# A graph layer with a gated delta rule: the chunk inverse carries L·T from level to level, key products in one, outputs behind the state

## The reference, cut to what matters

```python
def step(S, x):
    qt, kt, vt, bt, gt = x
    S = S * jnp.exp(gt)[..., None, None]
    kv = jnp.einsum('bhk,ebhkv->ebhv', kt, S)
    delta = (vt[None] - kv) * bt[..., None]
    S = S + kt[None, :, :, :, None] * delta[..., None, :]
    ot = jnp.einsum('bhk,ebhkv->ebhv', qt * scale, S)
    return (S, ot)
```

## Time and profile before

| | |
|---|---|
| three runs | 991.96, 995.42 (median), 997.62 us |
| span of the profiled execution | 993.7 us |
| PE busy | 894.7 us (90%), 12598 matmul records |
| DVE, ACT, POOL busy | 600.3, 254.6, 369.8 us |
| first transposes of the delta loop to its last output matmul | 562.8 to 924.6 us |

### The profile page before, as it was taken

One profiled execution on the slowest core, in us unless ns is written; L12 is line 12 of the kernel. 1 busy time (PEld: TensorE's weight loads), 2 busy tenths in 40 slices (PEclk: granted clock), 3 DMA queues, 4 the chain that ended last, 5 costly groups with the idle time before them and its releaser, 6 DMA issues.

```text
span 993.7 us, 28569 instructions
## 1 busy us (share of the span) xinstructions
PE 894.7 (90%) x12598; PEld 577.6 (58%) x12598; DVE 600.3 (60%) x1288; ACT 254.6 (26%) x502; POOL 369.8 (37%) x303
## 2 busy tenths in 40 slices
PE   3999999999998999999999888888888888888598
PEld 1454453445665444444444478788788788887343
DVE  7799999958884323236075555545555555554274
ACT  1121112201221000032122244333333343333331
POOL 5021100000111200002899576564565646542582
PEclk9999999999999999999999999999999999999989
DMA  8300000120000600000166843433434334321452
GB/s 258 121 1 1 1 1 1 43 63 1 1 2 3 231 1 1 0 1 2 16 244 258 275 124 99 124 105 94 117 99 120 99 101 118 99 57 35 116 145 65
DMA packets 74869, 80.59 MB, mean 81 GB/s; under 512 B 34437, under 2 KB 57655, under 8 KB 74743
## 3 DMA queue, kind: packets, MB, share of 16 engines
q1 hardware_dynamic: 69623, 57.58, 21.1%
q0 software_dynamic: 5120, 21.14, 6.0%
HBM read 54.25 MB, written 24.39 MB: 79 GB/s over the span
## 4 chain that ended last, share of the span: by engine, by line
PE 68%; POOL 11%; DVE 9%; issue 8%; DMA 1%; ACT 1%; SPq 0%; DVEq 0%; POOLq 0%
PE bank L829 16%; PE bank L760 9%; PE bank L530 7%; PE bank L563 4%; PE bank L549 3%; POOL nrm L1274 3%; POOL qkv_slots L1279 2%; PE bank L751 2%; DVE rows L1570 2%; PE bank L930 2%; PE bank L1003 2%; PE bank L919 2%; POOL gb_slots L1269 2%; PE bank L906 2%; PE bank L944 2%
## 5 line engine op out<-in xcount | busy, mean ns | idle before, releaser
L751 PE MATMUL bank<-W,xT 128*128 128x512 f32 x296 | 128.3, 593 | 0.0
L751 PEld LDWEIGHTS bank<-W,xT 128*128 128x128 f32 x296 | 56.0, 190 | 69.9 <-issue 69.7
L829 PE MATMUL bank<-big 64*64 64x64 f32 x2240 | 84.6, 222 | 6.4 <-issue 5.5
L760 PE MATMUL bank<-hs,big 125*125 125x512 f32 x200 | 86.6, 593 | 0.0
L829 PEld LDWEIGHTS bank<-big 64*64 64x64 f32 x2240 | 75.9, 137 | 8.2 <-issue 7.2
L530 PE MATMUL bank<-W,xT 128*125 128x512 f32 x160 | 79.3, 615 | 0.0
L1255 POOL TENSOR_TENSOR big<-big,ident_sb 125x125 f32<-125x125 f32 x10 | 11.4, 1141 | 173.9 <-ACT big L1066 173.9
L829 PE MATMUL bank<-tB 64*64 64x64 f16 x2560 | 59.5, 195 | 16.8 <-issue 12.2
L1314 POOL TENSOR_TENSOR tB<-tA,masks_sb 128x512 f16<-128x512 f16 x20 | 39.3, 1967 | 92.8 <-DVE tA L1816 92.8
L1831 DVE TENSOR_TENSOR tB<-bank,masks_sb 128x512 f16<-128x512 f32 x80 | 54.7, 684 | 21.2 <-PE bank L829 21.1
L760 PEld LDWEIGHTS bank<-hs,big 125*125 125x125 f32 x200 | 37.3, 188 | 47.7 <-issue 47.5
(11 more groups left out here) (302 smaller groups left out, 1874.1 us busy)
## 6 DMA issues: line engine op xcount, KB each, us to landing
big<-qkv_slots SPq DMA_DIRECT2D x40, 256.0 KB, 3.6
rows<-step_rows SPq DMA_DIRECT2D x40, 128.0 KB, 3.5
rows<-gam_rows SPq DMA_DIRECT2D x40, 128.0 KB, 3.3
big<-qkv_slots SPq DMA_DIRECT2D x80, 64.0 KB, 2.7
big<-qkv_slots SPq DMA_DIRECT2D x40, 128.0 KB, 3.0
o_slots<-big SPq DMA_DIRECT2D x40, 128.0 KB, 2.5
x_all<-in_x SPq DMA_DIRECT2D x10, 224.0 KB
out<-tC SPq DMA_DIRECT2D x10, 224.0 KB
```

The costliest lines, as they stand in the source:

```text
L751: last = mm(bank[:, b0, :], xT[:, k, t * P:t * P + 128], W[:, w, k, :], start=(k == 0), stop=(k == KC - 1))
L760: last = mm(bank[0:P, t % 2, :], cnt[:, s, t * P:(t + 1) * P], hs[:, s, :], start=(s == 0), stop=(s == NT - 1))
L829: last = mm(bank[q, b0, a * CL:(a + 1) * CL], lhsT[q, a, :], rhs[q, a, :], start=True, stop=True)
```

## The change

1. **Inverse.** `untranspose` and `level_m` of level 1 are gone. `pairs` is now two DVE operations: `TT16` by a mask, and `B16[0]` by DVE's transposition of 32x32 blocks. `first_m` forms L·T, `first_mt` its transpose; from then on M = L·T is carried: `level_up` forms the next M from M's transpose (`MT16`) and `B`, and in the same step the next `TT16` and `MT16` side by side with one 128-wide product for a matmul. Only the last level forms T itself. ACT's two copies for a level become one of 1024 columns (`keep_tm`), and for level 3 one of 512.
2. **Key products.** `kBD` holds the keys of two heads on the diagonal of a 128x128 matrix (zeroed once by DVE, refilled by two ACT copies on 64 partitions for a unit); 8 matmuls of 128x128x128 against keys and queries side by side replace the 32 of `key_key` and `key_query`.
3. **Outputs.** `outputs` is split into `state_part` and `out_part`; the outputs of a unit's second chunk are made one round later, and SP has a round more.
4. **Orders.** The rounds of all engines are rewritten; POOL no longer makes `TT16`; `T0`, `TT` and `RES` have one buffer in place of two.

```diff
+            def key_products(u):
+                s = u % 2
                 pe.wait_ge(S["kF_done"], u + 1)
+                pe.wait_ge(S["qF_done"], u + 1)
+                for a in range(8):
+                    last = mm(pair_of_banks(s, a), kBD[:, a, :], kqF[s][:, a, :, :].rearrange("p w n -> p (w n)"), start=True, stop=True)
+                last.then_inc(S["kk_psum"], 1)
...
+            def level_up(u, lv):
+                s = u % 2
+                B = B16[lv % 2][s]
+                pe.wait_ge(S["b_done"], level_count(u, lv))
+                pe.wait_ge(S["tm_done"], level_count(u, lv))
+                products(MB[s], MT16[s], B).then_inc(S["m_psum"], 1)
+                if lv == LEVELS - 2:
+                    products(TTB[s], B, TT16[s]).then_inc(S["tm_psum"], 1)
                 else:
-                    pe.wait_ge(S["t_done"], level_count(u, lv - 1))
-                products(MB[s], AT16[s], T16[s]).then_inc(S["m_psum"], 1)
+                    for a in range(8):
+                        for b in range(2):
+                            q = slice(CL * b, CL * b + CL)
+                            last = mm(pair_of_banks(s, a)[q, :], B[q, a, :], TM[s][q, a, :, :].rearrange("p w n -> p (w n)"), start=True, stop=True)
+                    last.then_inc(S["tm_psum"], 1)
...
             for h in range(NSC + 2):
+                unit_of(level_up, h - 1, 3)
+                unit_of(key_products, h)
                 chunk_of(old_keys, h, 0)
+                unit_of(last_level, h - 1)
+                if h >= 3:
+                    out_part(2 * (h - 3) + 1)
                 chunk_of(solve, h, 0)
+                unit_of(residual, h - 1)
+                chunk_of(state_part, h, 0)
+                unit_of(first_m, h)
+                unit_of(features, h + 1)
+                unit_of(first_fix, h - 1)
+                unit_of(first_mt, h)
                 chunk_of(old_keys, h, 1)
+                unit_of(level_up, h, 1)
                 chunk_of(solve, h, 1)
                 unit_of(second_fix, h - 1)
+                chunk_of(out_part, h, 0)
+                chunk_of(state_part, h, 1)
+                unit_of(level_up, h, 2)
+            out_part(NCK - 1)
...
+                for b in range(2):
+                    q = slice(CL * b, CL * b + CL)
+                    A(kBD[q, :, q], bank[q, TB[s], :].rearrange("p (a n) -> p a n", n=CL), ACT.Copy)
...
+            def keep_tm(u, lv):
+                s = u % 2
+                act.wait_ge(S["tm_psum"], level_count(u, lv + 1))
+                if lv == LEVELS - 2:
+                    A(TT16[s], bank[:, TTB[s], :].rearrange("p (a n) -> p a n", n=CL), ACT.Copy).then_inc(S["tm_done"], 1)
+                else:
+                    A(TM[s].rearrange("p (z a) w n -> p z (a w n)", z=2), bank[:, TB[s]:TTB[s] + 1, :], ACT.Copy).then_inc(S["tm_done"], 1)
...
+            def pairs(u):
...
+                V.tensor_tensor(TT16[s], AT16[s], bm(level0T, 8), ALU.mult).then_inc(S["tt1_done"], 1)
+                dve.wait_ge(S["tt1_done"], u + 1)
+                V.transpose(B16[0][s], TT16[s]).then_inc(S["t16_done"], 1)
```

More of the change, by code:

```diff
@@ L257, in gps_layer @@
         vp = [unit(big, 16 + s) for s in range(2)]
-        kF = [unit(big, 22 + s) for s in range(2)]
-        qF = [unit(xTu, s) for s in range(2)]
+        kqF = [buf[:, n * D:(n + 2) * D].rearrange("p (a w n) -> p a w n", w=2, n=CL) for buf, n in ((big, 22), (xTu, 0))]
+        kF, qF = ([f[:, :, w, :] for f in kqF] for w in range(2))
+        kBD = big[:, 5 * D:7 * D].rearrange("p (a n) -> p a n", n=2 * CL)
         kG = [[unit(xTu, 2 + 2 * p + s) for s in range(2)] for p in range(2)]
@@ L471, in _ @@
                 load_kp(0, c)
-            for h in range(NSC + 2):
+            for h in range(NSC + 3):
                 if h + 2 < NSC:
@@ L871, in level_t, with first_mt @@
[L871 to L877, removed]
+                pe.wait_ge(S["t16_done"], u + 1)
+                products(MB[s], AT16[s], B16[0][s]).then_inc(S["m_psum"], 1)
+            def first_mt(u):
+                s = u % 2
+                pe.wait_ge(S["pt_done"], u + 1)
+                products(TB[s], B16[0][s], AT16[s]).then_inc(S["tm_psum"], 1)
@@ L878, in level_t, with last_level @@
+            def last_level(u):
+                s, lv = u % 2, LEVELS - 1
+                B = B16[lv % 2][s]
                 pe.wait_ge(S["b_done"], level_count(u, lv))
-                products(TB[s], TT16[s], B16[s]).then_inc(S["t_psum"], 1)
-                products(TTB[s], B16[s], TT16[s]).then_inc(S["tt_psum"], 1)
+                pe.wait_ge(S["tm_done"], level_count(u, lv))
+                products(TB[s], TT16[s], B).then_inc(S["t_psum"], 1)
+                products(TTB[s], B, TT16[s]).then_inc(S["tt_psum"], 1)
@@ L896, in second_fix @@
                 pe.wait_ge(S["uu_done"], u + 1)
-                products(MB[s], RES[s], UU[s]).then_inc(S["tf_psum"], 1)
+                products(MB[s], RES, UU).then_inc(S["tf_psum"], 1)
             def old_keys(c):
@@ L921, in solve, with state_part @@
                 last.then_inc(S["z_psum"], 1)
-            def outputs(c):
+            def state_part(c):
                 u, c2 = c // 2, c % 2
@@ L1830, in level_b @@
                 dve.wait_ge(S["m_psum"], level_count(u, lv))
-                V.tensor_tensor(B16[s], pm(MB[s]), bm(level[lv], 8), ALU.mult).then_inc(S["b_done"], 1)
+                V.tensor_tensor(B16[lv % 2][s], pm(MB[s]), bm(level[lv], 8), ALU.mult).then_inc(S["b_done"], 1)
             def residual(u):
@@ L1871, in _ @@
                 gate_rows(t)
+            dve.wait_ge(S["first_scattered"], 64)
+            dve.wait_ge(S["rest_scattered"], 32 * (NT - 2))
+            V.memset(kBD, 0.0).then_inc(S["filled"], 1)
             for h in range(NSC + 2):
-                unit_of(level_b, h - 1, 3)
+                unit_of(level_b, h - 1, 4)
                 unit_of(lower, h)
@@ L1876, in _ @@
                 unit_of(lower16, h)
-                unit_of(decay_matrix, h + 1)
-                unit_of(level_b, h - 1, 4)
-                unit_of(pairs, h)
-                chunk_of(new_state, h, 0)
-                chunk_of(right_side, h, 1)
-                unit_of(level_b, h, 1)
-                unit_of(scores, h)
-                unit_of(residual, h - 1)
-                unit_of(first_fix, h - 1)
-                unit_of(level_b, h, 2)
-                chunk_of(new_state, h, 1)
-                unit_of(second_fix, h - 1)
+                unit_of(pairs, h)
+                unit_of(residual, h - 1)
+                chunk_of(new_state, h, 0)
+                unit_of(scores, h)
+                unit_of(level_b, h, 1)
+                unit_of(first_fix, h - 1)
+                chunk_of(right_side, h, 1)
+                unit_of(level_b, h, 2)
+                unit_of(second_fix, h - 1)
+                chunk_of(new_state, h, 1)
+                unit_of(decay_matrix, h + 1)
+                unit_of(level_b, h, 3)
             def mix_rows(t):
```

165 lines of the change are left out of this document (72 added, 93 removed).

## The result

The changed kernel takes **1016.75 us** (median of 4 runs, 1014.31 to 1025.99); the kernel before took 993.69 beside it. The ratio is 1.0257 with a 95% interval of 1.0214 to 1.0299 (the quotient of the two medians alone is 1.023): 2.6% slower, where 1.0% faster was forecast and 1003 was the range's upper end. The profiled execution has a span of 1015.9 us against 993.7.

A forecast was written before the change was run, and what follows sets the result against it. PE was taken as bound by its number of instructions; a unit of 17.0 us instead of 17.8 gave 993.7 - 12.5 + 2 + 0.5 = 983.7 span, so 985.4 us, range 970 to 1003.

The forecast's parts named there:

- code bounds the loop before: Delta loop before: PE bound by arriving instructions, 127 matmul records per 4.2 us, 17.7 us a unit.
- PE's work: PE's own issue time in a unit of the changed loop: 13.7 us, against 13.9 before.
- Key products: PE's 16 new float32 records of 128x128 in a unit: 2.0 us, against 1.92 before.
- wait A: PE before level_up 1, waiting for ACT's copy MT16: 1.1 us a unit.
- wait B: PE before level_up 3, waiting for DVE's level 3 mask and ACT's 1024-wide copy: 1.8 us a unit.
- the edit at nothing: TT16's mask and the block transposition on DVE: 0.68 us each, done 0.7 before first_m, little cost in the steady part.
- wait C: PE before first_m, waiting for DVE's block transposition: not forecast, 0.60 us in the changed kernel's trace.
- 0.4 a unit for pauses: PE's stops for code in the changed loop: about one in a unit, 0.4 us.
- clock rival: Two waits a unit bring the clock to 0.91 all through the loop: unit 18.4, kernel about 1007 us; chance 0.13.
- the 17.0: Forecast length in us of a unit of the changed loop, 0.8 less than before.
- the start, +2: First rounds: kBD copies, qF and DVE's operations lengthen the hand-overs; 2 us more, bounds 0 and +4.
- the end, +0.5: Last round: 0.5 us more for the late state_part; last outputs otherwise at 0.

The follow-up runs named there:

- run with half the columns: Kernel before the change, with the 64x64x64 products of the inverse cut to 32 columns; 1010.32 us, ratio 1.023.
- all three edits: Changed kernel with add_eye released behind DVE's mask, second_fix between level_up 2 and 3, key products one head at a time without kBD; 966.28 us, ratio 0.973.
- first edit: Changed kernel with POOL's add_eye waiting for TT16 instead of AT16; 998.81 us, ratio 1.0069.
- waits filled: Changed kernel with seven unused matmuls in the first round, plus one each in wait A and wait B of each round; 997.52 us, ratio 1.007.
- all three edits and the filled start: Kernel with all three edits, plus seven unused matmuls of 512 float32 columns in the first round alone; 963.0 us, ratio 0.9707.
- run with the filled start: Changed kernel as it is, plus seven unused matmuls of 512 float32 columns in its first round; 1009.08 us, ratio 1.016.

## Why the prediction was wrong

**Right: code bounds the loop before, and the number of records sets it.** The run with half the columns does not show this by its time, since PE's issue time hardly fell in it. What shows it are the stops, 126 or 127 records apart in the earlier trace rows and with half the columns alike, and the kernel with all three edits: 378 records in 12.58 us with a wait among them, and units of 15.1 and 15.2 for 456 records.

**Right: PE's work, waits A and B.** Key products 2.0 against 2.0. Counted by issue as the forecast was: work 13.8 against 13.7, wait A 1.3 against 1.1, wait B 1.7 against 1.8.

**Wrong, and the largest part: the edit at nothing.** "On DVE the mask lasts 0.68 ... Both end 0.7 us before PE comes to `first_m`." It lasts 1.79, since POOL's `add_eye` is released by the same semaphore and reads SBUF at the same time. The upper bound of 2.0 was named, but got no price; 1.1 us more against a slack of 0.7 is already a wait, and the rest of wait C is hand-over. The forecast had 16.6 for a unit without a stop for code (13.7 + 1.1 + 1.8); it is 17.55. Of these 0.95 us, wait C is 0.8, so 16 x 0.8 = 13 us, and the first edit gave back just that (17.55 to 16.76). The Trainium skill (SBUF — State Buffer, Who interferes with whom) says that a DVE instruction with two SBUF inputs and a GpSimd one that reads SBUF block one another, and that the one that starts first keeps the port for its whole length. The trace agrees in each order: DVE ends 0.55 after POOL when POOL is first, and where DVE was first, in the first round (the pair of rows from 569 us), it took 0.69 and POOL 1.77 instead of 1.27. I had not applied that rule.

**Wrong: 0.4 a unit for pauses.** That is 6.4 us for the 16 units; what they take beyond 16 x 17.55 is 292.6 - 280.8 = 11.8. The four units of 18.2 to 18.4, each with one stop for code, hold 2.9 of it: a stop comes in every second unit and not in each, but wait B follows it in full. The three late units of 20.0, 20.2 and 21.4 hold 8.8. The clock rival named such dips, at 0.91 all through; they came as a few deep ones (0.98 over the stretch), no more than before had in its own 16 units, but they did not go away as the 17.0 assumed. The kernel before has 284.1 - 16 x 17.2 = 8.9 beyond its clean unit of the earlier trace rows, so the forecast also let part of the old pauses vanish without a reason.

**Wrong: the start, +2.** It is +9.0. With the waits filled it is 39.3 at clock 1.00, so 4.9 of the 9.0 belong to the clock (0.85 in the changed kernel); 4.1 are left, just above the upper bound of +4, and the kernel before was itself at 0.95. Dropping the block-diagonal part alone gives 39.5, at clock 0.83, so this part with its two copies lies on the path, as forecast. Of those 4.7 us less, its own price is about what the forecast had: at full clock the first two units take 9.1 and 14.4 with it (filled waits), 7.8 and 13.1 without it (all three edits and the filled start; the first unit takes 7.8 without the other two edits as well), 1.2 and 1.3 against the forecast's 1.5 in each.

**Wrong: the end, +0.5.** It is +5.7. The kernel before had clock 1.00 there and the changed one 0.96. With the changed kernel's own waits but at clock 1.00 (the run with the filled start) it is 45.7, so 2.5 of the 5.7 go with the clock. The filled waits can't tell: they end ahead of the last rounds, and the end is 48.3 at 0.96 there too. With waits B and C reduced, at clock 1.00, it is 43.5, so these two are 2.2; about 1 us is open.

By these steps the miss in the loop is 33.2 us (+23.2 instead of -10.0): 7.0 at the start, 5.2 at the end, 21.0 in the units. Of the 21.0, 15.2 are the unit without a stop (16 x 0.95, most of it wait C, then wait A), 5.4 the pauses (11.8 against 6.4), and 0.4 rounding in the forecast. That the kernel might be slower had a chance of 0.14, put down to the clock; the chief cause was the wait that had been set at nothing.

**By part of the change.** The levels' part has fewer records and one hop, as forecast; it was not tried alone. The block-diagonal product saves 16 records a unit, 0.5 us of code by 4.2 us for 127, and costs two copies on ACT, 1.0, ahead of the one PE waits for; without it the kernel is 29.5 us faster. The new place of `second_fix` opened wait B: moved, it gives 21.4. `TT16` on DVE met POOL: parted, it gives 17.9. All three put right give 50.5 and not the sum of 68.8, since what bounds the loop then is code, and the rest of the change is then worth 2.7% against the kernel before.

## What to carry to other kernels

Write down for each term whether it stands in every unit or only in some: here the unit without a stop and the pauses of the others missed by different amounts, for different reasons. Before an operation is moved to VectorE with both inputs in SBUF, look at what the same semaphore releases on GpSimd; a few hundredths of a microsecond decided here which of the two waited for the other, DVE for 1.1 us or POOL for 0.5. Once an engine that was bound by its code gets fewer instructions, each new hand-over has to be covered by other work, or the gain turns into idle time. And before a run with less work is read, look at whether the work became less: half the columns left the pitch of the records as it was.

## What the runs showed of the hardware

- *A kernel gets faster by useless work.* Seven unused matmuls in the first round took the granted clock there from 0.82 to 1.00 and the stretch from 38.3 to 34.6 us; two more in each round took the changed kernel, with those seven in, from 1009.08 to 997.52, and from 1016.75 without any.
- *Fewer columns can be slower.* 32 columns instead of 64 left the pitch of float32 records at 0.028 against 0.030 us, but the clock went from 0.98 to 0.91 over the 16 units and from 0.95 to 0.60 at the start, and the kernel took 18 us more.
- *Code arrives at a rate.* 126 or 127 matmul records, each with its weight load, for 4.2 us, in one kernel with and one without waits among them; a wait of 0.60 in 378 records cost nothing beside that.
- *The order of two starts decides the price.* A DVE operation of 0.69 took 1.79 when POOL's started 0.03 earlier; POOL's took 1.77 instead of 1.27 when DVE's was 0.04 earlier.
- *The block transposition on DVE* takes 0.71 for 128 x 512 float16, as long as a mask. By the figure of the Trainium skill (VectorE: DVE Perf Modes, The three transpose paths) the estimate was 1.24, which the trace does not bear out here.
